# Retention scores in groups that fill four PSUM banks, values of eight heads in one visit, and a new order of work for all engines

## The chip, the cores and the metric

The kernel runs on one NeuronCore of one Trainium2 chip. The metric is the time of one execution on the device in microseconds. All arithmetic is float32.

## The reference, cut to what matters

The input x has 32 sequences of 256 tokens with 128 channels. A first block (L0) normalises x, computes an attention over 128 channels, multiplies it by a gate and adds it to x. A second block (L1) does the same with a retention of 16 heads (width 8 for queries and keys, 16 for values) and with a soft mixture of 8 experts as its gate:

```python
scores = einsum('bhtd,bhsd->bhts', q, k) * mask          # mask: decay, causal, 16 heads
denom  = clip(abs(scores).sum(-1, keepdims=True), 1.0, 50000.0)
ret    = einsum('bhts,bhsv->bthv', scores / denom, v)
ret    = ret * rsqrt(mean(ret * ret, -1) + EPS)
s      = ((xn @ W_g + b_g) * ret) @ W_o + b_o
logits = einsum('bnd,esd->bnes', xn, slots)               # 8 experts x 64 slots
dispatch, combine = softmax(logits, over n), softmax(logits, over all slots)
h   = gelu(einsum('besh', dispatched slots, w1) + b1);  eo = h @ w2 + b2
out = x + s * silu(einsum('bmd,bnm->bnd', eo, combine))
```

Only the retention's scores and values are computed in another grouping after the change; the rest keeps its instructions and gets another place in the order.

## The kernel before

The kernel works on pairs of sequences (512 tokens), 16 pairs in all. Every piece of work on a pair is a small function that issues a few instructions on one engine: `xnT`, `s`, `e`, `score`, `PT`, `local`, `r`, `k`, `v` are the L0 matmuls, `qk`, `gT`, `vg`, `quad`, `g`, `ms`, `o` those of the retention, `LT`, `mxT`, `rB`, `DT`, `slots`, `h`, `eo`, `out` those of the experts. The table `ORDER` (line 53) lists for each of TensorE (PE), VectorE (DVE), ScalarE (ACT) and GpSimd (POOL) the pieces in the order in which that engine issues them, each with an age: in step n of the loop the piece is done for pair n minus age. The loop (`steps_of`) has 18 steps, so a pair is spread over up to three steps and each engine always has three pairs in hand. Every engine is a queue in this written order; a piece waits on semaphores for its inputs (`ready[...]`, `filled[...]`), and whatever stands behind it on its engine waits too. Four PSUM banks of 512 columns (`banks`) are shared out by the table `BANK`; `claim` makes a matmul wait until the last reader of the bank's earlier content is done. The other four banks are one tensor, `bank_s`, for the retention's scores.

The retention of a pair has 32 units (2 sequences x 16 heads), four of them to a quad, 8 quads. Keys are masked by GpSimd into `km`, one 128 x 256 tile a quad (`km_`, line 315), four buffers. `quad` (line 995) makes the scores of four heads: the four heads sit in four groups of 32 rows of the array and write into four banks; for keys 0 to 127 the moving side has 256 queries, for keys 128 to 255 the later 128, so 384 columns of each bank are filled. `ret_` (line 656) multiplies the 4 x 384 columns by the causal mask into `ret`, `ab` (line 476) takes the absolute value into `ret_abs`, `add` (line 323) adds the two key blocks' absolute values on GpSimd. `g` (line 1007) then makes the values (two phases, from `ret`) and the row sums (one phase, from `ret_abs`) of the quad in four groups of 32 columns; two quads share a bank, and `usq`, `den`, `ug`, `rx` read that bank. `ret` and `ret_abs` have two buffers (`MR`), `bank_s` has one: the next `quad` waits for `ret`.

Pieces the text speaks of later: `xn2` (DVE) normalises for L1, `rstd2` and `rnorm` (POOL) its factors, `LTm`, `drec` (DVE), `DTe`, `Dc` (ACT) and `dn` (POOL) make the dispatch softmax before `DT` turns it, `hb` (DVE) adds the bias before `hg` (ACT, Gelu) and `eo` (PE), `eoc` (DVE) takes expert outputs out, `ce` is an Exp, `ln` and `rs` are Ln and Exp of the retention's norm, `tr`, `tv`, `sp`, `zt` are Tanh, `field`, `rvg`, `mix` are DVE instructions with two tensor inputs.

Of the kernel before, what the change touches and what calls it, by code (L numbers as in the profile page):

```python
# [1128 lines left out]
```

## Time and profile before

| | |
|---|---|
| median of 3 runs | 1090.27 us (1090.27 to 1090.41) |
| the profiled execution | 1089.83 us, span 1088.0 us |
| busy of the span | PE 1048.5, weight loads 828.0, DVE 919.0, ACT 806.6, POOL 387.3 us |
| granted TensorE clock | 0.995 over the span |

The span runs from the first to the last instruction. Busy time of PE is modelled from pipelined matmuls, so a high share says that PE always had something in hand, not that it streams at its peak. A float32 matmul of the program is two instructions (passes) in the trace. The profile's page and the answers of the trace give engine, line of the kernel, tiles and shapes for each group.

### The profile page before, as it was taken

Reading aid. Unit: us, or ns where it says so; the run is one execution under the profiler, and the core shown is the slowest. Engines: PE = TensorE matmul, PEld = TensorE weight load, DVE = VectorE, ACT = ScalarE, POOL = GpSimd, SP = SyncE. Lnnn points to the kernel's source line nnn. Section 1 sums busy time; section 2 is a strip of 40 time slices with the busy share of each in tenths; the row PEclk is TensorE's granted clock in tenths of the full one; section 3 lists DMA queues with packets and bytes.
Section 4 is the critical chain, followed back from the end, with each engine's and each line's share of the span. In section 5 each row is a group of like instructions: output and inputs, shape, how many; then the busy total and the mean of one; then the engine's idle time right before and its main releaser. Section 6 shows DMA issues by size and latency. Waiting matters only on the chain.

```text
span 1088.0 us, 27272 instructions
## 1 busy us (share of the span) xinstructions
PE 1048.5 (96%) x10244; PEld 828.0 (76%) x10244; DVE 919.0 (84%) x1818; ACT 806.6 (74%) x1434; POOL 387.3 (36%) x555
## 2 busy tenths in 40 slices
PE   5799999999999999999999999999999999999997
PEld 3478787787878778787786877778787787877866
DVE  3788888988889888997988889888998888989785
ACT  4487877778777786877778777887777868777775
POOL 2432533334343332433335233343433324333240
PEclk9899999999999999999999999999999999999999
DMA  6000000000000000000000000000000000000000
GB/s 257 11 11 2 11 11 2 21 2 11 11 2 21 2 11 11 3 20 2 21 1 12 11 2 20 2 11 11 2 21 2 15 7 11 12 1 12 2 11 11
DMA packets 18463, 16.85 MB, mean 15 GB/s; under 512 B 800, under 2 KB 17440, under 8 KB 18080
## 3 DMA queue, kind: packets, MB, share of 16 engines
q1 hardware_dynamic: 18336, 15.12, 4.3%
q8 instruction: 84, 1.38, 0.5%
q14 instruction: 43, 0.35, 0.1%
HBM read 10.93 MB, written 4.19 MB: 14 GB/s over the span
## 4 chain that ended last, share of the span: by engine, by line
PE 90%; DVE 5%; issue 4%; POOL 1%; ACT 1%; DVEq 0%; POOLq 0%; ACTq 0%
PE bank L969 11%; PE bank L979 11%; PE bank L1023 10%; PE bank_s L1000 7%; PE bank L989 6%; PE bank L960 5%; PE bank L930 5%; PE bank L952 3%; PE bank L910 3%; PE bank L1038 3%; PE bank L825 3%; PE bank L1030 3%; PE bank L876 3%; PE bank L923 3%; PE bank L856 2%
## 5 line engine op out<-in xcount | busy, mean ns | idle before, releaser
L326 POOL TENSOR_TENSOR ret_abs<-ret_abs 128x512 f32<-128x512 f32 x128 | 168.3, 1315 | 435.9 <-ACT ret_abs L479 435.9
L659 DVE TENSOR_TENSOR ret<-bank_s,k_sb 128x1536 f32<-128x1536 f32 x128 | 224.1, 1751 | 5.0 <-PE bank L1023 2.2
L479 ACT ACTIVATE ret_abs<-ret 128x1536 f32<-128x1536 f32 x128 | 189.1, 1477 | 0.5 <-DVE ret L659 0.5
L474 ACT ACTIVATE hact<-hact 128x512 f32<-128x512 f32 x128 | 80.1, 626 | 86.5 <-DVE hact L728 86.1
L979 PE MATMUL bank<-w_sb,hact 128*128 128x128 f32 x1024 | 132.0, 277 | 0.0
L969 PE MATMUL bank<-slotsT,w_sb 128*128 128x128 f32 x1024 | 130.7, 278 | 0.9 <-ACT slotsT L469 0.9
L979 PEld LDWEIGHTS bank<-w_sb,hact 128*128 128x128 f32 x1024 | 124.1, 192 | 8.9 <-ACT hact L474 4.3
L969 PEld LDWEIGHTS bank<-slotsT,w_sb 128*128 128x128 f32 x1024 | 120.6, 192 | 10.2 <-issue 6.6
L1023 PE MATMUL bank<-ret,vrow 128*32 128x256 f32 (+1 forms) x2048 | 108.3, 329 | 0.0
L728 DVE TENSOR_TENSOR hact<-bank,v_sb 128x512 f32<-128x512 f32 x128 | 87.6, 685 | 11.7 <-PE bank L979 8.2
L333 POOL TENSOR_SCALAR dT<-dT,drec 128x256 f32<-128x256 f32 x128 | 64.5, 517 | 91.7 <-DVE drec L723 91.7
L1000 PE MATMUL bank_s<-qT,km 32*128 32x256 f32 x1024 | 91.4, 426 | 0.4 <-issue 0.3
L1023 PEld LDWEIGHTS bank<-ret,vrow 128*32 128x32 f32 x2048 | 59.9, 109 | 41.6 <-issue 2.5
L320 POOL TENSOR_SCALAR km<-kT,k_sb 128x256 f32<-128x256 f32 x128 | 60.0, 483 | 76.7 <-DVE kT L645 76.7
L1023 PE MATMUL bank<-ret_abs,k_sb 128*32 128x256 f32 x1024 | 78.7, 379 | 0.0
L440 ACT ACTIVATE cT<-bank 128x512 f32<-128x512 f32 x64 | 38.2, 598 | 50.5 <-PE bank L930 50.4
L1000 PEld LDWEIGHTS bank_s<-qT,km 32*128 32x128 f32 x1024 | 40.1, 183 | 36.5 <-issue 30.9
L989 PE MATMUL bank<-eorow,cT 128*128 128x129 f32 x512 | 63.9, 278 | 1.0 <-issue 1.0
L455 ACT ACTIVATE dT<-cT,ltmax 128x256 f32<-128x256 f32 x128 | 64.5, 517 | 0.0
L989 PEld LDWEIGHTS bank<-eorow,cT 128*128 128x128 f32 x512 | 59.5, 191 | 3.0 <-issue 1.2
L960 PE MATMUL bank<-d,xn 128*128 128x512 f32 x128 | 57.7, 593 | 0.3 <-ACT d L462 0.3
L462 ACT ACTIVATE d<-bank 128x512 f32<-128x512 f32 x64 | 38.1, 595 | 23.9 <-PE bank L952 23.9
(143 smaller groups left out, 2307.1 us busy)
## 6 DMA issues: line engine op xcount, KB each, us to landing
x_sb<-x SPq DMA_DIRECT2D x16, 256.0 KB, 2.8
w_sb<-w SPq DMA_DIRECT2D x2, 2048.0 KB, 14.2
out<-attn SPq DMA_DIRECT2D x16, 256.0 KB, 2.3
v_sb<-vectors SPq DMA_DIRECT2D x1, 705.0 KB, 7.5
k_sb<-consts SPq DMA_DIRECT2D x1, 538.0 KB, 6.3
w_sb<-weights SPq DMA_DIRECT2D x1, 512.0 KB, 5.0
w_sb<-weights SPq DMA_DIRECT2D x1, 320.0 KB, 3.3
slot_sb<-slot_rows SPq DMA_DIRECT2D x1, 256.0 KB, 3.5
```

What stands on the lines that cost most here:

```text
L326: pool.tensor_tensor(both[:, :, P:SEQ], both[:, :, P:SEQ], both[:, :, SEQ:3 * P], ALU.add)\
L333: ins = pool.tensor_scalar(dT[:, m % 2, b], dT[:, m % 2, b], drec[:, m, b:b + 1], 1.0, ALU.mult, ALU.mult)
L474: act.activation(hact[:, e % 2], hact[:, e % 2], ACT.Gelu).then_inc(ready["hg"].sem, 1)
L479: act.activation(ret_abs[:, q % MR], ret[:, q % MR], ACT.Abs).then_inc(ready["ab"].sem, 1)
L659: dve.tensor_tensor(ret[:, q % MR], bank_s[:, :, 0:3 * P], causal.unsqueeze(1).broadcast_to([P, Q, 3 * P]), ALU.mult)\
L728: dve.tensor_tensor(hact[:, e % 2], bank[:].rearrange("p (c n) -> p c n", c=HC), V["b1"][:, e * HC:(e + 1) * HC].unsqueeze(2).broadcast_to ...
L960: ins = pe.matmul(bank[:], xn3[:, j], d[:, j], start=(i == 0), stop=(i == 1))
L969: ins = pe.matmul(bank[:, c * P:(c + 1) * P], w1_sb[:, e, c * P:(c + 1) * P], slotsT[:, e // 2, 2 * (e % 2):2 * (e % 2) + 2].rearrange("p ...
L979: ins = pe.matmul(bank[:, i * C:(i + 1) * C], hact[:, i, c], w2_sb[:, e, c], start=(c == 0), stop=(c == HC - 1))
L989: ins = pe.matmul(bank[:, i * (C + 1):(i + 1) * (C + 1)], cT[:, m, j * P:(j + 1) * P], eorow[:, m, b], start=(m == 0), stop=(m == E // 2 - 1))
L1000: pe.matmul(bank_s[:, n, 0:SEQ], km[rows, q % KM, 0:P], qT[par][rows, b], start=True, stop=True)
L1023: ins = pe.matmul(bank[n * HT:(n + 1) * HT, into[0]:into[1]], left, src[:, q % MR, n, cols[0]:cols[1]], start=(i == 0 and phase == 0), sto ...
```

## The change

The quads are replaced by six score groups a pair (`scores`, named A in the order). For each sequence the first group holds the 128-key-by-128-query blocks of keys 128 to 255 of all four quads (16 matmuls of 128 columns), the second and third hold the blocks of keys 0 to 127 of two quads each (8 matmuls of 256 columns). Each group fills 4 x 512 columns. `ret`, `ret_abs` become `low`, `low_abs` (4 quads) and `high`, `high_abs` (2 quads), one buffer each. `add` now adds two quads at once (1024 elements a partition), four times a pair. `values` (named gg) issues what two `g` issued, without a break, after one wait.

`ORDER` and `BANK` are written anew for all four engines. `h` 4 to 7, `eo` 2 to 5, the last score group and the last values move from age 2 to age 1, `xn2` and `rstd2` from age 1 to age 0.

```diff
+GROUPS, HALVES = 6, 4
...
-    "PE": [("quad", 7, 2), ("h", 4, 2), ("eo", 2, 2), ("eo", 3, 2), ("h", 5, 2), ("h", 6, 2), ("eo", 4, 2),
...
+    "PE": [("ms", 3, 2), ("xn2T", 0, 1), ("eo", 6, 2), ("qk", 0, 1), ("eo", 7, 2), ("qk", 1, 1), ("xn3T", 0, 1),
+           ("out", 0, 2), ("out", 1, 2), ("LT", 0, 1), ("xnT", 0, 0), ("A", 0, 1), ("LT", 1, 1), ("LT", 2, 1),
+           ("LT", 3, 1), ("A", 1, 1), ("o", 0, 2), ("gT", 0, 1), ("vg", 0, 1), ("vg", 1, 1), ("DT", 0, 1),
+           ("gT", 1, 1), ("DT", 1, 1), ("o", 1, 2), ("s", 0, 0), ("A", 2, 1), ("gg", 0, 1), ("DT", 2, 1),
+           ("DT", 3, 1), ("k", 0, 0), ("global", 0, 0), ("slots", 0, 1), ("ms", 0, 1), ("slots", 1, 1),
+           ("mxT", 0, 1), ("A", 3, 1), ("h", 0, 1), ("gg", 1, 1), ("e", 0, 0), ("h", 1, 1), ("r", 0, 0),
+           ("A", 4, 1), ("rB", 0, 1), ("h", 2, 1), ("ms", 1, 1), ("eo", 0, 1), ("eo", 1, 1), ("h", 3, 1),
+           ("score", 0, 0), ("srow", 0, 0), ("score", 1, 0), ("A", 5, 1), ("gg", 2, 1), ("PT", 0, 0),
+           ("PT", 1, 0), ("v", 0, 0), ("h", 4, 1), ("eo", 2, 1), ("eo", 3, 1), ("local", 0, 0), ("h", 5, 1),
+           ("h", 6, 1), ("ms", 2, 1), ("gg", 3, 1), ("eo", 4, 1), ("eo", 5, 1), ("h", 7, 1)],
+    "DVE": [("hb", 7, 2), ("rx", 3, 2), ("stat", 0, 0), ("xn3", 0, 1), ("eoc", 3, 2), ("qkc", 0, 1), ("qkc", 1, 1),
...
+            ("cs", 0, 1), ("eoc", 0, 1), ("hb", 3, 1), ("smax", 0, 0), ("cs", 1, 1), ("smax", 1, 0),
+            ("srowc", 0, 0), ("ka", 0, 0), ("cs", 2, 1), ("cs", 3, 1), ("ret", 5, 1), ("x2", 0, 2), ("srec", 0, 0),
+            ("rv", 0, 0), ("den", 2, 1), ("hb", 4, 1), ("eoc", 1, 1), ("ug", 2, 1), ("rvg", 0, 0), ("field", 0, 0),
+            ("hb", 5, 1), ("prod", 0, 0), ("x1", 0, 0), ("stat2", 0, 0), ("rx", 2, 1), ("den", 3, 1), ("ug", 3, 1),
+            ("hb", 6, 1), ("xn2", 0, 0), ("eoc", 2, 1)],
+    "ACT": [("dsq", 3, 2), ("hg", 6, 2), ("xn2Tc", 0, 1), ("hg", 7, 2), ("ln", 0, 2), ("xn3Tc", 0, 1),
+            ("rs", 0, 2), ("LTc", 0, 1), ("DTe", 0, 1), ("LTc", 1, 1), ("xnTc", 0, 0), ("LTc", 2, 1), ("ab", 0, 1),
+            ("LTc", 3, 1), ("DTe", 1, 1), ("gTb", 0, 1), ("ab", 1, 1), ("gTb", 1, 1), ("DTe", 2, 1), ("Dc", 0, 1),
+            ("sT", 0, 0), ("DTe", 3, 1), ("Dc", 1, 1), ("zt", 0, 2), ("usq", 0, 1), ("Dc", 2, 1), ("Dc", 3, 1),
+            ("ab", 2, 1), ("slc", 0, 1), ("slc", 1, 1), ("dsq", 0, 1), ("kr", 0, 0), ("hg", 0, 1), ("sgT", 0, 0),
+            ("usq", 1, 1), ("eTc", 0, 0), ("ab", 3, 1), ("hg", 1, 1), ("tr", 0, 0), ("dsq", 1, 1), ("rBc", 0, 1),
+            ("ab", 4, 1), ("hg", 2, 1), ("hg", 3, 1), ("P", 0, 0), ("P", 1, 0), ("ce", 0, 1), ("usq", 2, 1),
+            ("PTc", 0, 0), ("PTc", 1, 0), ("ab", 5, 1), ("tv", 0, 0), ("dsq", 2, 1), ("hg", 4, 1), ("sp", 0, 0),
+            ("hg", 5, 1), ("ce", 1, 1), ("usq", 3, 1), ("ce", 2, 1), ("ce", 3, 1)],
+    "POOL": [("rnorm", 0, 1), ("rstd", 0, 0), ("km", 0, 1), ("km", 1, 1), ("km", 2, 1), ("km", 3, 1),
+             ("mixa", 0, 0), ("dn", 0, 1), ("dn", 1, 1), ("add", 0, 1), ("dn", 2, 1), ("dn", 3, 1), ("km", 4, 1),
+             ("km", 5, 1), ("km", 6, 1), ("km", 7, 1), ("add", 1, 1), ("add", 2, 1), ("add", 3, 1), ("rstd2", 0, 0)],
...
             def add(p, par, h):
+                b, half = divmod(h, 2)
+                pool.wait_ge(*ready["ab"](p, 3 * b))
+                pool.wait_ge(*ready["ab"](p, 3 * b + 1 + half))
+                pool.tensor_tensor(high_abs[:, :, :, P:SEQ], high_abs[:, :, :, P:SEQ], low_abs[:, :, 2 * half:2 * half + 2], ALU.add)\
...
-            def quad(p, par, q):
+            def scores(p, par, a):
+                b, i = divmod(a, 3)
+                quads = range(Q * b, Q * b + Q) if i == 0 else range(Q * b + 2 * i - 2, Q * b + 2 * i)
                 pe.wait_ge(*ready["qkc"](p, 0))
+                pe.wait_ge(*ready["km"](p, quads[-1]))
+                since(pe, ready["ret"], *((p, a - 1) if a else (p - 1, GROUPS - 1)))
+                for u, q in enumerate(quads):
+                    for n in range(Q):
+                        rows = slice(n * HT, (n + 1) * HT)
+                        if i == 0:
+                            ins = pe.matmul(bank_s[:, n, u * P:(u + 1) * P], km[rows, q % KM, P:SEQ], qT[par][rows, b, P:SEQ],
+                                            start=True, stop=True)
+                        else:
+                            ins = pe.matmul(bank_s[:, n, u * SEQ:(u + 1) * SEQ], km[rows, q % KM, 0:P], qT[par][rows, b],
+                                            start=True, stop=True)
+                ins.then_inc(filled["A"].sem, 1)
```

## Rows read from the trace of the kernel before

**Rows 1.** The page, busy time, and the chain that ended last by engine.
```profile
PE 1048.5 (96%) x10244; PEld 828.0 (76%) x10244; DVE 919.0 (84%) x1818; ACT 806.6 (74%) x1434; POOL 387.3 (36%) x555
...
PE 90%; DVE 5%; issue 4%; POOL 1%; ACT 1%; DVEq 0%; POOLq 0%; ACTq 0%
```

**Rows 2.** The waits: who waited for whom, us in total, times, longest.
```profile
PE bank L952 <- POOL dT L333: 12.5, 14, 0.9
```

**Rows 3.** Timeline of PE, 66 us from the middle: start, length, what, times.
```profile
560.60 1.03 PE L916 MATMUL bank<-w_sb,xn2T 128*128 128x256 f32 x4
...
567.40 0.59 PE L930 MATMUL bank<-xn3T,snT 128*128 128x256 f32 x2
567.83 0.59 PE L930 MATMUL bank<-xn3T,slot_sb 128*128 128x256 f32 x2
568.36 0.71 PE L1000 MATMUL bank_s<-qT,km 32*128 32x256 f32 x8
568.89 0.40 PE L1003 MATMUL bank_s<-qT,km 32*128 32x128 f32 x8
569.22 0.70 PE L930 MATMUL bank<-xn3T,snT 128*128 128x256 f32 x2
569.76 0.59 PE L930 MATMUL bank<-xn3T,slot_sb 128*128 128x256 f32 x2
...
575.03 0.86 PE L1023 MATMUL bank<-ret,vrow 128*32 128x256 f32 x16
...
576.79 0.61 PE L1023 MATMUL bank<-ret_abs,k_sb 128*32 128x256 f32 x8
578.29 0.66 PE L952 MATMUL bank<-k_sb,dT 128*128 128x128 f32 x4 [0.89 <-POOL dT L333]
...
609.77 0.69 PE L1030 MATMUL bank<-usq,k_sb 128*128 128x256 f32 x2
610.39 0.71 PE L1000 MATMUL bank_s<-qT,km 32*128 32x256 f32 x8
...
626.40 1.03 PE L916 MATMUL bank<-w_sb,xn2T 128*128 128x256 f32 x4
```

**Rows 4.** Groups by line and shape: busy us, mean ns of one, idle before.
```profile
L659 DVE TENSOR_TENSOR ret<-bank_s,k_sb 128x1536 f32<-128x1536 f32 x128 | 224.1, 1751 | 5.0 <-PE bank L1023 2.2 <-PE bank_s L1003 1.4
L479 ACT ACTIVATE ret_abs<-ret 128x1536 f32<-128x1536 f32 x128 | 189.1, 1477 | 0.5 <-DVE ret L659 0.5
L326 POOL TENSOR_TENSOR ret_abs<-ret_abs 128x512 f32<-128x512 f32 x128 | 168.3, 1315 | 435.9 <-ACT ret_abs L479 435.9
...
L728 DVE TENSOR_TENSOR hact<-bank,v_sb 128x512 f32<-128x512 f32 x128 | 87.6, 685 | 11.7 <-PE bank L979 8.2 <-PE bank L969 2.4
...
L449 ACT ACTIVATE cT<-cT 128x512 f32<-128x512 f32 x64 | 39.8, 622 | 0.2
...
L588 DVE SCALAR_TENSOR_TENSOR spin<-bank,srec,srow 128x128 f32<-128x128 f32 x64 | 18.0, 344 | 8.5 <-PE bank L876 8.5
...
L406 ACT ACTIVATE spin<-spin,v_sb 128x512 f32<-128x512 f32 x16 | 11.3, 708 | 1.6 <-DVE spin L588 1.6
```

**Rows 5.** Timeline of ACT around its table loads.
```profile
550.53 0.61 ACT L474 ACTIVATE hact<-hact 128x512 f32<-128x512 f32 x1
551.16 1.28 ACT L449 ACT_TABLE_LOAD   x1
552.46 0.63 ACT L449 ACTIVATE cT<-cT 128x512 f32<-128x512 f32 x1
...
555.95 0.37 ACT L489 ACTIVATE usq<-bank 128x256 f32<-128x256 f32 x1
556.81 0.42 ACT L493 ACTIVATE den<-den 128x256 f32<-128x256 f32 x1 [0.49 <-DVE den L666]
```

**Rows 6.** Timeline of DVE and POOL: instructions that overlap an `add`, and one that doesn't.
```profile
550.03 2.07 DVE L628 TENSOR_SCALAR xn<-x,mv,rstd 128x128 f32<-128x128 f32 x4
...
550.70 1.31 POOL L326 TENSOR_TENSOR ret_abs<-ret_abs 128x512 f32<-128x512 f32 x1 [1.70 <-ACT ret_abs L479]
...
11.21 1.41 DVE L557 SCALAR_TENSOR_TENSOR mix<-xnT,v_sb,mix 128x512 f32<-128x512 f32 x2 [3.54 <-POOL mix L294]
...
574.02 2.15 DVE L557 SCALAR_TENSOR_TENSOR mix<-xnT,v_sb,mix 128x512 f32<-128x512 f32 x2
```

**Rows 7.** Timeline of PE in the last step, from its last `eo`.
```profile
1074.94 1.16 PE L979 MATMUL bank<-w_sb,hact 128*128 128x128 f32 x8
...
1082.23 1.16 PE L1038 MATMUL bank<-w_sb,ug 128*128 128x128 f32 x8 [0.43 <-DVE ug L687]
```

More of the change, by code:

```diff
@@ L169, in build @@
         qT, kT = ([sb(f"{n}_{i}", 2, SEQ) for i in range(2)] for n in ("qT", "kT"))
-        KM, MR = 4, 2
+        KM = 4
         km = sb("km", KM, SEQ)
         vrow, grow = sb("vrow", TILES, HEADS, HT), sb("grow", 2, TOK)
-        ret, ret_abs = sb("ret", MR, Q, 3 * P), sb("ret_abs", MR, Q, 3 * P)
+        low, low_abs = sb("low", Q, Q, P), sb("low_abs", Q, Q, P)
+        high, high_abs = sb("high", Q, 2, SEQ), sb("high_abs", Q, 2, SEQ)
         usq, den = sb("usq", 2, SEQ), sb("den", 2, SEQ)
@@ L211, in build @@
             ("prod", 1), ("x1", 1), ("stat2", 1), ("mv2", 1), ("var_eps2", 1), ("rstd2", 1), ("rn", 3), ("rnorm", 1),
-            ("xn2", 1), ("xn3", 1), ("xn2Tc", 1), ("xn3Tc", 1), ("qkc", 2), ("km", QUADS), ("vgc", 2), ("gTb", 2), ("ret", QUADS),
-            ("ab", QUADS), ("add", QUADS), ("usq", DUOS), ("den", DUOS), ("dsq", DUOS), ("ug", DUOS),
+            ("xn2", 1), ("xn3", 1), ("xn2Tc", 1), ("xn3Tc", 1), ("qkc", 2), ("km", QUADS), ("vgc", 2), ("gTb", 2), ("ret", GROUPS),
+            ("ab", GROUPS), ("add", HALVES), ("usq", DUOS), ("den", DUOS), ("dsq", DUOS), ("ug", DUOS),
             ("rx", DUOS), ("ln", 1), ("rs", 1), ("gated", 2), ("attn", 2), ("LTc", 4), ("mx", 3), ("rmax", 1), ("rBc", 1), ("cs", 4), ("ce", 4),
@@ L474, in hg, with ab @@
                 act.activation(hact[:, e % 2], hact[:, e % 2], ACT.Gelu).then_inc(ready["hg"].sem, 1)
[L476 to L479 removed]
+            def ab(p, par, a):
+                b, i = divmod(a, 3)
+                act.wait_ge(*ready["ret"](p, a))
+                if i == 0:
+                    since(act, ready["add"], *((p, 1) if b else (p - 1, 3)))
+                    ins = act.activation(low_abs[:], low[:], ACT.Abs)
+                else:
+                    h = 2 * b + i - 1
+                    since(act, filled["gg"], *((p, h - 1) if h else (p - 1, HALVES - 1)))
+                    ins = act.activation(high_abs[:], high[:], ACT.Abs)
+                ins.then_inc(ready["ab"].sem, 1)
             def gTb(p, par, u):
@@ L991, in out_ @@
                 ins.then_inc(filled["out"].sem, 1)
-            def quad(p, par, q):
-                b = q // Q
+            def scores(p, par, a):
+                b, i = divmod(a, 3)
+                quads = range(Q * b, Q * b + Q) if i == 0 else range(Q * b + 2 * i - 2, Q * b + 2 * i)
                 pe.wait_ge(*ready["qkc"](p, 0))
-                pe.wait_ge(*ready["km"](p, q))
-                since(pe, ready["ret"], *((p, q - 1) if q else (p - 1, QUADS - 1)))
-                for n in range(Q):
-                    rows = slice(n * HT, (n + 1) * HT)
-                    pe.matmul(bank_s[:, n, 0:SEQ], km[rows, q % KM, 0:P], qT[par][rows, b], start=True, stop=True)
-                for n in range(Q):
-                    rows = slice(n * HT, (n + 1) * HT)
-                    ins = pe.matmul(bank_s[:, n, SEQ:3 * P], km[rows, q % KM, P:SEQ], qT[par][rows, b, P:SEQ],
-                                    start=True, stop=True)
-                ins.then_inc(filled["quad"].sem, 1)
@@ L1010, in g, with values @@
+                ins.then_inc(filled["A"].sem, 1)
+            def values(p, par, h):
+                b, half = divmod(h, 2)
+                pe.wait_ge(*ready["add"](p, h))
                 pe.wait_ge(*ready["vgc"](p, b))
-                bank = banks[BANK["g", q - 1]] if i else claim("g", p, q)
+                bank = claim("gg", p, h)
                 spread = vrow[:].rearrange("p j h v -> p j (h v)")
-                for phase in range(3):
-                    for n in range(Q):
-                        src = (ret, ret_abs)[phase // 2]
-                        sblock = phase % 2
-                        at = (Q * (q % Q) + n) * HT - i * VD
-                        left = spread[:, 2 * b + sblock, at:at + HT] if phase < 2 else K["count"][:, (1 - i) * VD:(1 - i) * VD + HT]
-                        cols = (0, SEQ) if sblock == 0 else (SEQ, 3 * P)
-                        into = (phase // 2 * SEQ + sblock * P, (phase // 2 + 1) * SEQ)
-                        ins = pe.matmul(bank[n * HT:(n + 1) * HT, into[0]:into[1]], left, src[:, q % MR, n, cols[0]:cols[1]],
-                                        start=(i == 0 and phase == 0), stop=(i == 1 and phase == 2))
@@ L1025, in g @@
-                ins.then_inc(filled["g"].sem, 1)
+                for i in range(2):
+                    for phase in range(3):
+                        for n in range(Q):
+                            at = (Q * (2 * half + i) + n) * HT - i * VD
+                            left = spread[:, 2 * b + phase, at:at + HT] if phase < 2 else K["count"][:, (1 - i) * VD:(1 - i) * VD + HT]
+                            right = (high[:, n, i], low[:, n, 2 * half + i], high_abs[:, n, i])[phase]
+                            into = ((0, SEQ), (P, SEQ), (SEQ, 2 * SEQ))[phase]
+                            ins = pe.matmul(bank[n * HT:(n + 1) * HT, into[0]:into[1]], left, right,
+                                            start=(i == 0 and phase == 0), stop=(i == 1 and phase == 2))
@@ L1027, in ms @@
+                ins.then_inc(filled["gg"].sem, 1)
             def ms(p, par, h):
@@ L1029, in ms @@
                 pe.wait_ge(*ready["ug"](p, h))
-                pe.matmul(banks[BANK["g", 2 * h]][:, SEQ:], K["heads"], usq[:, h % 2], start=True, stop=True)\
+                pe.matmul(banks[BANK["gg", h]][:, SEQ:], K["heads"], usq[:, h % 2], start=True, stop=True)\
                   .then_inc(filled["ms"].sem, 1)
@@ L1056, in _ @@
                           "local": local, "r": r, "k": k_, "v": v, "xn2T": xn2T_, "xn3T": xn3T_, "qk": qk, "vg": vg, "LT": LT,
-                          "mxT": mxT, "rB": rB_, "DT": DT, "slots": slots, "h": h, "eo": eo, "out": out_, "quad": quad, "g": g,
+                          "mxT": mxT, "rB": rB_, "DT": DT, "slots": slots, "h": h, "eo": eo, "out": out_, "A": scores, "gg": values,
                           "gT": gT, "ms": ms, "o": o}, ORDER["PE"],
```

79 lines of the change are left out of this document (35 added, 44 removed), and 33 rows, old and new, of tables (BANK, ORDER).

## The prediction

> **What bounds the kernel now.** I read the page's busy line and the chain first [rows 1]: TensorE is busy for 1048.5 of 1088 us, and 90% of the chain that ended last runs over it. VectorE (84%) and ScalarE (74%) are not the bound, but every piece hands its result through them. Then the waits [rows 2]: in the steady part TensorE waits for one thing, the turning of dT (`DT` 0), 14 times, 12.5 us in all. Then the timeline of a whole step [rows 3]. The same instruction (`vg` 0) starts at 560.60 and 626.40, so a step takes 65.80 us. Of these 0.96 pass between the expected start of `DT` 0 and its actual one: `g` 1 ends its issue at 576.79 + 0.54, `DT` starts at 578.29 (the row says 0.89 idle). About 0.3 more are gaps that busy time hides, such as 0.62 from `ms` 2 (609.77) to `quad` 7 (610.39), where other matmuls of that shape take 0.43 and an entry into a quad 0.10. So TensorE's own stream is 64.54 us a step, 98% of it.
>
> **TensorE's stream after the change.** The rows show what a visit to the small tiles costs [rows 3]. Two full-array matmuls of 256 columns start 0.43 apart (567.40, 567.83). From the last of them to the quad it is 0.53: 0.10 to enter. The quad takes from 568.36 to 569.22, 0.86, where its four passes of four concurrent matmuls stream 2 x 0.216 + 2 x 0.108 = 0.65 (0.216 is half of 0.43); 0.21 are its first, exposed weight load and the drain at its end (256-column part 0.53 instead of 0.43, 128-column part 0.33 instead of 0.22). The next full matmul takes 0.54 instead of 0.43: 0.10 to come back (I take 0.056, half of it, where a transpose follows, whose own start needs less; the bounds are 0 and 0.10).
> - A low group has 8 passes of 128 columns: 8 x 0.109 + 0.215 = 1.09. A high group has 4 of 256: 4 x 0.216 + 0.215 = 1.08. Six groups: 2 x 1.09 + 4 x 1.08 = 6.49, against 8 x 0.865 = 6.92: -0.43. This holds if weight loads within a group stay hidden, as from the 256- to the 128-column part now. The bound from above is a quad's own parts repeated: 0.33 for each quad of a low group, 0.53 for each of a high one, 2 x 1.32 + 4 x 1.17 = 7.3: +0.4. I take the first, since within one visit only the first pass of a quad shows an exposed load.
> - Visits: before, 9 a step (five lone quads, three quads with a `g` pair, one lone pair), 6 of them left into matmuls and 3 into transposes: 9 x 0.093 + 6 x 0.10 + 3 x 0.056 = 1.61. After, from the order, 8: A0, A1, A3, A4, A2+gg0, A5+gg2, gg1, gg3, left 5 times into matmuls and 3 into transposes: 1.42. That is -0.19.
> - The values: `g` pairs stood side by side already and ran without a break (575.03 to 577.33, 2.30), so one visit for eight heads gives nothing on TensorE.
> The stream becomes 64.54 - 0.43 - 0.19 = 63.92 us a step, for 16 pairs 9.9 us less.
> The Trainium skill says in TensorEngine Tiling (Array Packing), Key Properties, that changing the tiling mode drains the array; the rows agree, with 0.10 to enter and 0.10 to leave.
>
> **The other engines.** `ret_` costs 1751 ns for 1536 columns, and 685 for 512 (`hb`, also from PSUM) [rows 4]: 1.04 ns a column, 2.29 us for 2048. 8 x 1.75 - 6 x 2.29 = 0.3 us less on VectorE, beside TensorE. `ab`: 1477 for 1536 and 622 for 512, 0.83 ns a column, 1.90 for 2048: 0.4 less on ScalarE. `add` is four instead of eight, each 2.0 to 2.6 us (from proportional to the second half alone, to twice 1315 ns); I take 2.4. ScalarE's order mixes functions more. Now it loads tables five times a step, each 1.28 us, 1.29 from start to start, and the overlap of neighbours is lost too, 1.4 in all [rows 5]. In the new order changes away from Gelu's table and back stand at hg6, ln, rs, hg0, P, hg4, ce1: seven loads. Four more (`tr`, `hg` 2, `sp`, `hg` 5) come if Tanh doesn't run on Gelu's table, which the trace can't show, since there no Tanh follows a Gelu directly. I take seven, the end nearer to today's five: +2.8 us, with the other end +8.4. ScalarE goes from about 50.4 to 52.8 of 65 us.
> The Trainium skill (ScalarE: Activation LUTs, What ACT_TABLE_LOAD costs) gives 2.66 us for each switch with its drain. By it two more loads would be 5.3 us of ScalarE; the rows show 1.29, and I go by them.
>
> **The new waits.** I laid the new order out with these lengths, counting from the start of `ms` 3: A0 ends at 10.9, A1 starts at 13.7 and ends at 14.7, A2 starts at 21.9, gg0 at 23.0, A3 31.6 to 32.7, gg1 33.8, A4 38.9 to 40.0, A5 46.8 to 47.9, gg2 47.8, `local` ends at 56.4, gg3 58.8, `eo` 6 is due at 64.7.
> - Score to score: A1 needs `ret` 0, 10.9 + 0.2 + 2.3 = 13.4. Slack 0.3, the smallest; the others have over 3.
> - Score to values: hand-over 0.2, `ret` 2.3, `ab` 1.9, `add` 2.4, 6.8 in all. gg0 has 8.3 for it, gg1 10.8, gg2 7.8, gg3 10.9. What stands before `ab` 1 (`gTb` 0) and `add` 0 (`dn` 1) fits. They hold.
> - `DT`: `dn` 0 comes 4 us before `DT` 0, `dn` 1 1 us before `DT` 1. The wait of 0.96 goes. `slots` 0 behind `Dc` 3 has 0.1 of slack, the banks of A2's neighbour `s` (behind `gTb` 1) 0.3.
> - The seam of the step. From the end of `local` (56.4) ScalarE and VectorE must do, one after the other: `field` 4 x 0.28 (18.0 us for 64), 1.1, `sp` 0.7, `hg` 5 0.6, a load 1.3, `ce` 1 0.55, `usq` 3 0.3, `ce` 2 and 3 1.1, `dsq` 3 0.3, a load 1.4, `hg` 6 0.6 [rows 4, 5]: 8.0. `eo` 6 is due 8.3 later. But `field` stands behind `rvg`, which has two SBUF inputs, and that behind `add` 3. By my layout `ret` 5 ends at 52.4 (`cs` 2, `cs` 3, `ka` before it), `ab` 5 at 54.3, `add` 3 at 56.8, so `rvg` ends at 57.5 and `field` at 58.5, 1.0 late. `eo` 6 starts about 0.8 late, and behind it are `qk`, `out` and everything. `xn2`, also behind this, is 0.4 late for `xn2T`, inside the same delay.
> - The port. An instruction of VectorE with two SBUF inputs, or a fast one, stretches while an `add` runs: `mix` takes 2.15 beside one and 1.41 alone, and the four of `xn2` 2.07 [rows 6]. After the change an `add` blocks up to 2.4 us at once, four times. Outside the seam I find it beside `mx` and `cs` 1, each with cover, and price the rest at 0.2 on the path (0 to 1).
> The Trainium skill (SBUF — State Buffer, Terms, shared port pair) says the port is held exclusively for a whole instruction. The 0.74 us that `mix` loses agree, and the rule speaks against wider adds: half as many, each worst case twice as long.
> New waits are thus 0.8 + 0.2 + 0.1 for the thin seams, 1.1, against 1.26 before. A step becomes 63.92 + 1.1 = 65.0.
>
> **Ends.** The first 33 us are L0 alone in both. The new order puts `k` before `e`. In this start `mix` ends at 12.6 [rows 6], so `k` waits for nothing long but puts itself ahead of `e`, up to 2 us; ScalarE's one-time squares of the slots stand behind `eTc` and cover part of it. I take +0.5 between 0 and 2. The tail from the last `eo` (1074.94) to the end is the same chain of `eoc`, `out`, `z`, `zt`, `x2` (13.1 us [rows 7]); `o` has the same place in it.
>
> **Sum.** Stream -9.9, waits 15 steps x -0.16 = -2.4, ends +0.5, thin seams in step 16, where L0's work no longer covers, +0.5: -11.3. The profiled execution of 1089.83 becomes 1078.5; the median is 0.44 above the profiled time, so 1079.
>
> **Rivals.**
> 1. The seam closes (adds at 2.0, `field` on time) and only 0.2 of waits is left: step 64.1, -1.7 x 15, 1089.8 - 25.5 + 1 + 0.4 = 1066. For it: my chain is 8.0 of 8.3 without the port. Against: it leaves nothing for a late `ret` 5, and VectorE has three pieces ahead of that. Chance 0.15.
> 2. Slower: Tanh between two Gelus costs its own loads. `hg` 4, `sp`, `hg` 5 then carry two more loads, 2.8 us, in the chain that already ends last at the seam, so nearly all of it is on the path: step 65.0 + 2.6 = 67.6, +1.8 x 15 = +27, 1117. It decides as soon as `sp` has its own load; half of it would do. For it: ScalarE's order has 11 changes of function. Against: it needs a switch that no row of this trace has. 0.12. A smaller version: `add` and two-input instructions meet at three or four seams for 0.8 each instead of one; step 66.6, 1103. 0.09.
> 3. A new wait of the old one's size takes its place (a second thin seam opens by 0.7): 65.7 a step, about 1090. 0.07.
> 4. The wide groups don't hide their loads: +0.4 instead of -0.43, 0.8 a step more, 1092. 0.07.
> My forecast, 1079 with its own range 1071 to 1086, has 0.50.
>
> **Numbers.** No change is within 0.2% (2.2 us). Faster: forecast and rival 1 and a little of 3, 0.69. Same: 0.08. Slower: 0.23. The range 1064 to 1100 takes in rivals 1, 3 and 4 and leaves out the loads of Tanh and extremes, 0.2.
>
> **What would show it.** Right: score groups of 1.09 and 1.08 from start to next start, 8 visits; steps of about 65.0 us; no wait at `DT` 0; a wait of 0.8 at `eo` 6 for hact from ScalarE; seven loads a step (112 in all). Wrong: eleven loads, groups of 1.3, `add` over 2.6 us, or TensorE waiting for `ret_abs` at `gg`.

## The result, and the profile after

The changed kernel takes 1103.3 us (median of 4 runs, 1102.95 to 1105.08) beside 1090.27 for the kernel before (1089.97 to 1090.41): ratio 1.0124, 95% interval 1.0109 to 1.0139. It is slower, where 1079 was forecast, and outside the range. The profiled execution took 1103.20, span 1101.4.

The page of the kernel after, busy time and the chain [rows 1]; then TensorE's waits [rows 2]:
```profile
PE 1049.2 (95%) x10244; PEld 812.3 (74%) x10244; DVE 903.5 (82%) x1786; ACT 851.5 (77%) x1434; POOL 383.6 (35%) x491
...
PE 4%; DVE 1%; ACT 1%; issue 0%; POOL 0%; POOLq 0%; DVEq 0%; ACTq 0%
```
```profile
PE bank L844 <- DVE xn L639: 15.5, 16, 7.0
...
PE bank L1044 <- DVE spin L599: 4.3, 15, 0.3
PE bank L998 <- DVE eorow L758: 3.1, 15, 0.2
```
The chain breaks off after 6% of the span, so this time it tells nothing. In the waits the one of 12.5 us at `DT` is gone, and three have come at the seam of the step: `xn2T` (L844) for `xn2` on VectorE (15.5 less the 7.0 of the first pair, so 15 of 0.57), `gg` 3 (L1044) for `field` (L599), `eo` 6 (L998) for VectorE's `eoc`.

The timeline of PE after: a high group, a low group (each with the instruction behind it, for the pitch) and the seam [rows 3]:
```profile
584.18 1.15 PE L1025 MATMUL bank_s<-qT,km 32*128 32x256 f32 x16
585.25 0.64 PE L1044 MATMUL bank<-high,vrow 128*32 128x256 f32 x8
...
620.88 0.60 PE L1051 MATMUL bank<-usq,k_sb 128*128 128x256 f32 x2
621.75 0.64 PE L1044 MATMUL bank<-high,vrow 128*32 128x256 f32 x8 [0.28 <-DVE spin L599]
...
626.83 0.60 PE L1051 MATMUL bank<-usq,k_sb 128*128 128x256 f32 x2
627.98 0.66 PE L844 MATMUL bank<-k_sb,xn 128*128 128x128 f32 x4 [0.55 <-DVE xn L639]
628.85 1.13 PE L998 MATMUL bank<-w_sb,hact 128*128 128x128 f32 x8 [0.21 <-DVE eorow L758]
...
1054.87 1.17 PE L1022 MATMUL bank_s<-qT,km 32*128 32x128 f32 x32
1055.97 1.16 PE L988 MATMUL bank<-slotsT,w_sb 128*128 128x128 f32 x8
```
A high group takes 1.07, a low one 1.10. `ms` 3 starts at 560.76 in one step and 626.83 in the next: 66.07. That step, and the mean of steps 2 to 15 (65.97; steps are counted from 0 to 17), stand against 65.80. To split such a step into stream and waits I gave each piece its usual pitch (start to next start where nothing is waited for) and summed what was above it; before that gives 64.54 + 1.26, after 63.93 + 2.03.

| us of the span | before | after | change | forecast |
|---|---|---|---|---|
| stream of all steps | 1032.6 | 1022.9 | -9.7 | -9.9 |
| waits, steps 2 to 15 | 17.6 | 28.5 | +10.9 | -2.4 |
| first `xn2T` starts at | 32.85 | 36.76 | +3.9 | +0.5 with the next row |
| waits, step 1 | 4.80 | 5.92 | +1.1 | |
| waits, steps 16 and 17, with 1.6 of a lower clock (see the two buffers) | 9.97 | 17.15 | +7.2 | +0.5 |
| sum | | | +13.4 | -11.3 |

Groups of the kernel after by line and shape (busy, mean ns of one, idle before) [rows 4, 5]:
```profile
L330 POOL TENSOR_TENSOR high_abs<-high_abs,low_abs 128x1024 f32<-128x1024 f32 x64 | 158.2, 2472 | 369.4 <-ACT high_abs L489 369.4
L678 DVE TENSOR_TENSOR high<-bank_s,k_sb 128x2048 f32<-128x2048 f32 x64 | 146.5, 2289 | 27.3 <-PE bank L1044 17.6 <-PE bank_s L1025 9.6
L489 ACT ACTIVATE high_abs<-high 128x2048 f32<-128x2048 f32 x64 | 122.2, 1909 | 27.1 <-DVE high L678 25.0
...
L478 ACT ACT_TABLE_LOAD x48 | 61.6, 1283 | 0.9
...
L618 DVE SCALAR_TENSOR_TENSOR prob<-prob 128x512 f32<-128x512 f32 x16 | 25.8, 1613 | 0.7 <-ACT prob L426 0.7
```
The wide instructions have the lengths of the forecast (`add` 2.47, `ret` 2.29, `ab` 1.91), and the tables are loaded seven times a step. The last row is the loss: `rvg` takes 1.61 us in the mean, where its kind takes 0.68. The timelines of DVE and POOL at the seam show why [rows 6]:
```profile
618.91 1.66 DVE L618 SCALAR_TENSOR_TENSOR prob<-prob 128x512 f32<-128x512 f32 x1
620.49 1.11 DVE L599 SCALAR_TENSOR_TENSOR spin<-bank,srec,srow 128x128 f32<-128x128 f32 x4
```
```profile
617.66 2.36 POOL L330 TENSOR_TENSOR high_abs<-high_abs,low_abs 128x1024 f32<-128x1024 f32 x1 [8.11 <-ACT high_abs L489]
```
`add` 3 runs to 620.02. `rvg` starts at 618.91 and ends 0.55 after it. `field`, the next in VectorE's queue, starts at 620.49. `local`, which it reads, starts at 617.30 on TensorE, and in the first run below `field` starts 1.99 after `local` does; so here it is some 1.2 late, and `prod`, `x1`, `stat2`, `rstd2` and `xn2` follow it one by one.

### The profile page after: what moved, and what is told of

It is laid out like the page before. It is cut to its first block and busy times, and to the rows that moved or that the text cites. A ratio compares the mean times of both kernels' runs of the same rounds, so it can differ in the third digit from the quotient of the medians.

```text
span 1101.4 us, 27081 instructions
## 1 busy us (share of the span) xinstructions
PE 1049.2 (95%) x10244; PEld 812.3 (74%) x10244; DVE 903.5 (82%) x1786; ACT 851.5 (77%) x1434; POOL 383.6 (35%) x491
## 5 line engine op out<-in xcount | busy, mean ns | idle before, releaser
L330 POOL TENSOR_TENSOR high_abs<-high_abs,low_abs 128x1024 f32<-128x1024 f32 x64 | 158.2, 2472 | 369.4 <-ACT high_abs L489 369.4
L678 DVE TENSOR_TENSOR high<-bank_s,k_sb 128x2048 f32<-128x2048 f32 x64 | 146.5, 2289 | 27.3 <-PE bank L1044 17.6
L489 ACT ACTIVATE high_abs<-high 128x2048 f32<-128x2048 f32 x64 | 122.2, 1909 | 27.1 <-DVE high L678 25.0
L998 PEld LDWEIGHTS bank<-w_sb,hact 128*128 128x128 f32 x1024 | 122.6, 192 | 22.0 <-issue 13.8
L998 PE MATMUL bank<-w_sb,hact 128*128 128x128 f32 x1024 | 130.0, 278 | 3.6 <-DVE eorow L758 3.1
L673 DVE TENSOR_TENSOR low<-bank_s,k_sb 128x2048 f32<-128x2048 f32 x32 | 73.3, 2291 | 21.6 <-PE bank L1044 17.8
L1044 PE MATMUL bank<-high,vrow 128*32 128x256 f32 x1024 | 80.7, 385 | 5.4 <-DVE spin L599 4.3
L1044 PE MATMUL bank<-high_abs,k_sb 128*32 128x256 f32 x1024 | 79.5, 379 | 0.0
L1025 PE MATMUL bank_s<-qT,km 32*128 32x256 f32 x1024 | 73.3, 400 | 1.5 <-DVE low L673 1.5
L485 ACT ACTIVATE low_abs<-low 128x2048 f32<-128x2048 f32 x32 | 61.4, 1917 | 13.6 <-DVE low L673 13.6
L844 PE MATMUL bank<-k_sb,xn 128*128 128x128 f32 x256 | 40.7, 283 | 23.5 <-DVE xn L639 15.5
L844 PEld LDWEIGHTS bank<-k_sb,xn 128*128 128x128 f32 x256 | 31.5, 144 | 42.2 <-DVE xn L639 21.7
```

The costliest lines, as they stand in the source:

```text
L330: pool.tensor_tensor(high_abs[:, :, :, P:SEQ], high_abs[:, :, :, P:SEQ], low_abs[:, :, 2 * half:2 * half + 2], ALU.add)\
L489: ins = act.activation(high_abs[:], high[:], ACT.Abs)
L673: ins = dve.tensor_tensor(low[:].rearrange("p n i m -> p (n i) m"), flat.rearrange("p (u m) -> p u m", m=P), causal[:, 2 * P:3 * P].unsque ...
L678: ins = dve.tensor_tensor(high[:].rearrange("p n i m -> p (n i) m"), flat.rearrange("p (u m) -> p u m", m=SEQ), causal[:, 0:SEQ].unsqueeze ...
L844: ins = pe.transpose(bank[:, j * P:(j + 1) * P], src[:, j], ident)
L998: ins = pe.matmul(bank[:, i * C:(i + 1) * C], hact[:, i, c], w2_sb[:, e, c], start=(c == 0), stop=(c == HC - 1))
```

## The experiments

Step lengths are means of steps 2 to 15 of the profiled execution, times the medians; each ratio is to the kernel before on the same chip.

**One swap on VectorE.**
```diff
-            ("rv", 0, 0), ("den", 2, 1), ("hb", 4, 1), ("eoc", 1, 1), ("ug", 2, 1), ("rvg", 0, 0), ("field", 0, 0),
+            ("rv", 0, 0), ("den", 2, 1), ("hb", 4, 1), ("eoc", 1, 1), ("ug", 2, 1), ("field", 0, 0), ("rvg", 0, 0),
```


> The kernel after with one edit: on VectorE field goes ahead of rvg. Theory A (the port: rvg stands beside add 3 and stretches from 0.69 to 1.66 us, and field, which reads PSUM, waits behind it): in every step the 0.36 us before the last values visit goes, the waits at ms 3, xn2T and eo 6 (1.3 us together) shrink by 0.6 to 0.9, the step falls from 65.98 to about 64.9 and the time from 1103 to about 1087. Theory B (ScalarE's table loads at the seam are the bound): the step changes by less than 0.3 us, 1099 to 1103.

Measured: 1090.78 us (1089.04 to 1092.67), ratio 1.0012 [1.0003, 1.0022]; the step 65.01. The timeline of DVE in it:
```profile
611.75 1.13 DVE L599 SCALAR_TENSOR_TENSOR spin<-bank,srec,srow 128x128 f32<-128x128 f32 x4 [0.29 <-PE bank L895]
612.79 0.68 DVE L618 SCALAR_TENSOR_TENSOR prob<-prob 128x512 f32<-128x512 f32 x1
```
`field` reads PSUM and starts as soon as `local` is done; `rvg` comes after the `add` and takes 0.68. The wait at `gg` 3 (0.35 a step) is gone, and that at `xn2T` is 0.13 instead of 0.73 (`ms` 3 starts at 618.94 and `xn2T` at 619.50, where 0.43 is the usual pitch). So the order of two names in one list gives back 12.5 us; the step is now 0.79 shorter than before, and the longer ends use that up.

**A short add at the seam.** The fourth `add` of a pair works on an eighth of its elements; the rest of that sum is left out.
```diff
+                w = P // 8 if h == 3 else P
+                pool.tensor_tensor(high_abs[:, :, :, P:P + w], high_abs[:, :, :, P:P + w], low_abs[:, :, 2 * half:2 * half + 2, 0:w], ALU.add)\
```


> The kernel after, with the add of the last values of a pair (add 3) leaving out seven eighths of its elements, so that it holds the port for some 0.5 us instead of 2.36; the order is the one of the kernel after. Theory A (the port): rvg takes 0.69 again, the step falls by about 1.0 to 65.0, the time to about 1088. Theory B (table loads or GpSimd's own chain of rstd2): no change beyond 0.3 us a step.

Measured: 1091.84 us (1089.13 to 1092.14), ratio 1.0014 [1.0005, 1.0023], with `rvg` still ahead of `field`; the step 65.07, and 64.97 without step 7, which the part on two instructions that start together (below) explains. The row of `rvg`:
```profile
614.45 0.68 DVE L619 SCALAR_TENSOR_TENSOR prob<-prob 128x512 f32<-128x512 f32 x1
```
Moved out of the way or the `add` made short, the gain is the same: it is the meeting of the two that costs, not the order as such.

**Two buffers of `high` and `high_abs`.** To have room, one expert's w1 serves all eight; the others' are left out.
```diff
-        high, high_abs = sb("high", Q, 2, SEQ), sb("high_abs", Q, 2, SEQ)
+        high, high_abs = sb("high", 2, Q, 2, SEQ), sb("high_abs", 2, Q, 2, SEQ)
-                    since(dve, filled["gg"], *((p, h - 1) if h else (p - 1, HALVES - 1)))
+                    since(dve, filled["gg"], *((p, h - 2) if h >= 2 else (p - 1, HALVES - 2 + h)))
```


> The kernel after with two buffers each for high and high_abs, so that ret of a high group no longer waits for the values before it. To make room all experts use the first w1 (the others are left out). Theory A (single buffers cost mainly in step 16, where L0's work is gone): the steady step stays at 65.9 to 66.0, step 16 falls from 63.8 to about 61.5, the time by 2 to 3 us. Theory B (single buffers set the steady step): the step falls by 0.5 or more, the time by 8 or more.

Measured: 1114.39 us (1112.3 to 1114.56), ratio 1.0222 [1.0207, 1.0237]: slower by 11 us than the changed kernel. Step 16 fell from 63.78 to 61.26, but the steady step rose to 66.80. No theory had that. DVE, POOL and PE around it:
```profile
598.79 3.44 DVE L726 TENSOR_TENSOR mx<-mx,cT 128x512 f32<-128x512 f32 x2
```
```profile
599.32 2.38 POOL L330 TENSOR_TENSOR high_abs<-high_abs,low_abs 128x1024 f32<-128x1024 f32 x1 [1.47 <-ACT high_abs L489]
```
```profile
602.29 0.65 PE L957 MATMUL bank<-k_sb,mx 128*128 128x128 f32 x4 [0.61 <-DVE mx L726]
```
With its buffer free the second `add` starts 0.26 ahead of the second `mx`, and this takes 2.66 us instead of 0.69 (their two lengths by tile are 685 and 2655 ns); `mxT` waits for it.

Of the 2.5 us that step 16 fell, only 0.9 belong to the buffers. `h` 5 waits 1.10 instead of 2.00 there, while A4 still waits 1.49 and `gg` 2 1.18. The other 1.6 are TensorE's clock: in the profiled execution of the changed kernel the granted clock is 0.74 from 1075 to 1080 us and 0.92 from 1080 to 1085, so part of that stretch ran at 1.2 GHz and not at 2.4. The run with the old start (below) has the same order in this step, waits the same 2.00 at `h` 5, and keeps a clock of 1.00; its step 16 takes 62.17. Here are `h` 5 and 6 in the changed kernel, and in that run:
```profile
1077.24 3.59 PE L988 MATMUL bank<-slotsT,w_sb 128*128 128x128 f32 x16 [2.00 <-DVE eorow L758]
```
```profile
1077.09 2.02 PE L996 MATMUL bank<-slotsT,w_sb 128*128 128x128 f32 x16 [2.00 <-DVE eorow L770]
```

**The same with that add short** (its second `add` of a pair on an eighth, the rest of the sum left out too).
```diff
+                w = P // 8 if h == 1 else P
```


> The kernel with two buffers of high (one expert's w1 for all, the others' left out), and in it the second add of each pair on an eighth of its elements, the rest of that sum left out. In the trace of the two-buffer kernel the second instruction of mx took 2.66 instead of 0.69 us while that add ran (599.32 to 601.70), and the matmul mxT waited for it. Theory A (the port: the buffer's wait held add 1 off mx before, and without it the two meet): the wait of 0.78 at mxT goes, the steady step falls from 66.80 to 66.0, the kernel from 1114.4 to 1101 to 1104. Theory B (the earlier abs and ret of the two-buffer kernel push something else on ScalarE or VectorE ahead of mxT): mx takes 0.69 again but the step stays at 66.6 or more, 1112 to 1114.

Measured: 1102.71 us (1102.56 to 1102.97), ratio 1.0123 [1.0106, 1.014]; the step 65.97. The same two instructions:
```profile
593.07 1.56 DVE L727 TENSOR_TENSOR mx<-mx,cT 128x512 f32<-128x512 f32 x2
```
The second `mx` takes 0.77 here, and both together took 3.44 before. So the 11.7 us between the two runs were the meeting at the port. A wait that holds a GpSimd `add` back can be worth more than the buffer that takes the wait away.

**Two instructions that start together.** The changed kernel has this meeting too. In its steady steps the second `mx` starts 0.06 to 0.08 ahead of `add` 1 (592.09 and 592.15), keeps its 0.69, and the `add` is the one that takes longer, 2.84 instead of 2.36, for which TensorE doesn't wait. In step 7 the two start within 0.01 of each other. The `mx` came first there in the profiled executions of the changed kernel, the swap and the one with old order and banks, and the `add` in those of the short add, the old start and the five loads. A usual step of the kernel with five loads, then its step 7, on VectorE and GpSimd:
```profile
390.68 1.48 DVE L726 TENSOR_TENSOR mx<-mx,cT 128x512 f32<-128x512 f32 x2
455.75 3.67 DVE L726 TENSOR_TENSOR mx<-mx,cT 128x512 f32<-128x512 f32 x2
```
```profile
391.54 2.84 POOL L330 TENSOR_TENSOR high_abs<-high_abs,low_abs 128x1024 f32<-128x1024 f32 x1 [2.11 <-ACT high_abs L489]
456.54 2.34 POOL L330 TENSOR_TENSOR high_abs<-high_abs,low_abs 128x1024 f32<-128x1024 f32 x1 [2.11 <-ACT high_abs L489]
```
The second `mx` takes 2.88 there, `mxT` waits 1.21, and the step takes 66.43 instead of 65.0. So this order has a meeting whose winner is set by less than 0.1 us, and 1.4 us hang on it wherever it is lost. The three pieces moved below part the two by 0.7 us, and with them no step of this kind is left.

**The start in the old order.** Step 0 runs the L0 pieces in the order of the kernel before (`e` ahead of `k`, `PT` 0 ahead of `srow`), and `claim` waits for whoever really held the bank.
```diff
+START = {"PE": [("xnT", 0, 0), ("s", 0, 0), ("e", 0, 0), ("global", 0, 0), ("r", 0, 0), ("k", 0, 0), ("score", 0, 0),
...
-                for name, k, age in order:
+                for name, k, age in (ORDER if step else START)[engine]:
```


> The kernel after, but the first step, in which there is only L0 of the first pair, is issued in the order of the kernel before (e ahead of k, PT ahead of srow); each bank claim waits for the bank's actual last holder. Theory A (the new order of L0 costs 3.9 us once at the start): xn2T of the first pair starts at about 33.0 instead of 36.8, the time falls by 3.5 to 4, the steps stay at 65.98. Theory B (the start is hidden behind the loads of the experts' weights): no change beyond 0.5 us.

Measured: 1101.35 us (1100.98 to 1101.87), ratio 1.0107 [1.0092, 1.0122]. The first `xn2T` starts at 35.20: 1.56 of the 3.9 are the order. The step is 66.07, and 65.95 without step 7, in which the `mx` lost (67.38); step 16 is 62.17 at a full clock.

**And in the old banks.** Under the new `BANK` `PT` and `srow` share a bank, `v` and `local` another. Here the first pair's L0 pieces have those of before.
```diff
+BANK0 = {('PT', 0): 0, ('PT', 1): 2, ('e', 0): 3, ('global', 0): 0, ('k', 0): 0, ('local', 0): 1, ('r', 0): 1, ('s', 0): 1, ('score', 0): 1, ('score', 1): 2, ('srow', 0): 1, ('v', 0): 0, ('xnT', 0): 3}
```


> The kernel after with the first step in the order of the kernel before and also with that kernel's banks for L0 of the first pair (with the order alone, PT and srow shared a bank and so did v and local). Theory A (order and banks of L0 are the whole 3.9 us of the start): xn2T of the first pair starts at 32.9 and the span falls by 3.9 from 1101.4. Theory B (something else): it stays at 35.2, as with the order alone.

Measured once: 1097.54 us beside 1089.46 for before (no interval). The first `xn2T`, in the changed kernel, with the old order, and with order and banks:
```profile
36.76 1.11 PE L844 MATMUL bank<-k_sb,xn 128*128 128x128 f32 x4 [7.02 <-DVE xn L639]
```
```profile
35.20 1.12 PE L852 MATMUL bank<-k_sb,xn 128*128 128x128 f32 x4 [7.02 <-DVE xn L651]
```
```profile
33.14 1.12 PE L858 MATMUL bank<-k_sb,xn 128*128 128x128 f32 x4 [7.01 <-DVE xn L657]
```
The start is explained to 0.3 us: the order 1.6, the shared banks 2.1.

**Five table loads instead of seven.** On top of the swap, `ce` 1 and 2 stand behind `PTc` 1 and `ce` 3 behind `tv`, so no Exp parts two Gelus.
```diff
-            ("hg", 5, 1), ("ce", 1, 1), ("usq", 3, 1), ("ce", 2, 1), ("ce", 3, 1)],
...
+           ("PTc", 1, 0), ("ce", 1, 1), ("ce", 2, 1), ("ab", 5, 1), ("tv", 0, 0), ("ce", 3, 1), ("dsq", 2, 1),
```


> field ahead of rvg as before, and ScalarE's ce 1, 2, 3 moved ahead of hg 4, so that Gelu's table stays from hg 4 to hg 7: five table loads a step instead of seven. Theory A (VectorE's line to xn2 paces the step, ScalarE's loads matter only for eo 6): the wait behind xn2T (0.42 + 0.16) shrinks by up to 0.4, the step falls from 65.01 to 64.6 to 65.0. Theory B (the loads pace it): the step falls to 64.3 or below, the time to 1080.

Measured: 1088.71 us (1088.3 to 1090.5), ratio 0.9998 [0.9989, 1.0008]; ScalarE loads five times a step and the step stays 65.0 (65.11 with step 7, in which the `mx` lost) with the same waits. `eo` 6, which waited for ScalarE's `hact` in the swapped kernel, now waits as long for VectorE:
```profile
620.36 1.13 PE L998 MATMUL bank<-w_sb,hact 128*128 128x128 f32 x8 [0.20 <-ACT hact L478]
```
```profile
623.84 1.13 PE L998 MATMUL bank<-w_sb,hact 128*128 128x128 f32 x8 [0.20 <-DVE eorow L758]
```
Two loads less are 2.6 us of ScalarE a step and nothing on the path of the steady step. Step 16 takes 61.56 instead of 63.15 and step 17 14.72 instead of 15.08. But the whole 1.6 of step 16 arise in matmuls at a lower clock that only the profiled execution of the swapped kernel has (0.92 from 1060 to 1065 us and 0.73 to 1070, where the five-load kernel has 1.00), so 0.4 us in step 17 are what the loads gave back; how much of the 2.1 us between the medians is theirs stays open.

**Three pieces moved.** On top of that: `attn` 1 behind `drec` 2 (it stood ahead of what `DT` 3 waits for), `x2` behind `sg`, `dsq` 0 behind `Dc` 3.
```diff
-            ("vgc", 0, 1), ("vgc", 1, 1), ("attn", 1, 2), ("mx", 0, 1), ("LTm", 3, 1), ("drec", 2, 1),
...
+           ("vgc", 0, 1), ("vgc", 1, 1), ("mx", 0, 1), ("LTm", 3, 1), ("drec", 2, 1), ("attn", 1, 2),
```


> The kernel with few loads, and three pieces moved on VectorE and ScalarE into idle stretches: attn 1 behind mx 0, LTm 3 and drec 2 (it waited 1.9 us for o 1 with DT 3's inputs behind it), x2 out of the stretch ahead of xn2 to right behind sg, dsq 0 ahead of ab 2. Theory A (waits of the new order are seams, each ended by one late piece): the 0.24 at DT 3 and the 0.25 at ms 3 go, the step is 64.0 to 64.3, the time 1075 to 1078. Theory B (VectorE's whole load is the bound): the step stays above 64.8.

Measured: 1082.89 us (1081.96 to 1084.14), ratio 0.9942 [0.9927, 0.9957]. The step is 64.72, between the two theories: the 0.24 at `DT` 3 are gone, the 0.13 at `xn2T` behind `ms` 3 are not, and `eo` 6 still waits 0.42.

**All of it, with the old start** (the edits of the last three headings and of the two on the start together).
```diff
-                return banks[BANK[name, k]]
+                return banks[bank_at(name, k, p)]
```


> The kernel with the moved seams and with the start of the kernel before (order and banks in the first step). The two savings add up: 3.9 us less than that kernel, 1071 to 1074.

Measured: 1079.32 us (1078.64 to 1079.71), ratio 0.9906 [0.989, 0.9923]: the fastest whole version, under the kernel before and the changed one. The old start gave 3.6 here too; the expectation was too low because it counted on a shorter seam. Its page, and the seam on PE and DVE:
```profile
PE 1043.1 (97%) x10244; PEld 807.9 (75%) x10244; DVE 921.5 (85%) x1786; ACT 808.4 (75%) x1402; POOL 381.0 (35%) x491
```
```profile
614.27 0.60 PE L1065 MATMUL bank<-usq,k_sb 128*128 128x256 f32 x2
614.84 0.66 PE L858 MATMUL bank<-k_sb,xn 128*128 128x128 f32 x4
615.69 1.13 PE L1012 MATMUL bank<-w_sb,hact 128*128 128x128 f32 x8 [0.20 <-DVE eorow L776]
```
```profile
607.07 1.13 DVE L617 SCALAR_TENSOR_TENSOR spin<-bank,srec,srow 128x128 f32<-128x128 f32 x4 [0.47 <-PE bank L909]
```
What is left is a chain of hand-overs: VectorE sits idle for 0.47 until `local` is out of TensorE, and from `field` over `sp`, `prod`, `x1`, `stat2` and `rstd2` to `xn2` (613.67) every piece needs the one before. `local` earlier would shorten it, and so might `sp` ahead of `hg` 4, behind which it stands for 0.3 on ScalarE; neither was tried.

**All adds short in that version** (each on an eighth, the rest of the sums left out), to see what the port still holds.
```diff
+                w = P // 8
```


> The best kernel so far (field ahead of rvg, five table loads, three pieces moved, the old start), all four adds of a pair on an eighth of their elements, the rest of the sums left out: what is left of the port and of the length of add in it. Theory A (the adds now lie beside cover everywhere in the steady part; the step's last wait is the chain from local over field, stat2 and rstd2 to xn2): 64.6 to 64.72 a step, 1077 to 1079.5. Theory B (adds still stretch pieces on the path): the step falls to 64.3 or less, 1073 or less. Step 16 may gain up to 1 us in both, since there gg 1 and gg 2 wait for add.

Measured: 1077.81 us (1076.78 to 1078.66), ratio 0.9894 [0.9879, 0.9909]. The step is 64.71, the same; step 16 falls from 60.68 to 59.38. In the steady state four adds of 2.4 us now cost nothing.

**The grouping in the order of before.** The wide groups and eight-head visits laid, by my hand, into the order and banks of the kernel before (A0 to A2 where quads 0 to 2 stood, no work moved between ages; `e`, which stood behind `g` 1 and `DT` 0, was put ahead of `gg` 0).
```diff
...
+           ("qk", 1, 1), ("gT", 0, 1), ("vg", 0, 1), ("xn3T", 0, 1), ("out", 0, 2), ("A", 0, 1), ("out", 1, 2),
+           ("LT", 0, 1), ("LT", 1, 1), ("A", 1, 1), ("LT", 2, 1), ("xnT", 0, 0), ("LT", 3, 1), ("gT", 1, 1),
+           ("vg", 1, 1), ("s", 0, 0), ("A", 2, 1), ("e", 0, 0), ("gg", 0, 1), ("DT", 0, 1), ("global", 0, 0),
...
```


> Grouping alone: the two wide score groups and the eight-head value visits, laid into the order and the PSUM banks of the kernel before (A0 to A2 behind quads 0 to 2, DT0 ahead, field work as before, no early rope). Theory A (the grouping itself is worth its own stream, measured as 1032.6 to 1022.9 us, and the loss of the changed kernel comes from its new order): the stream falls by about 9.7 us, the waits stay near the 55.4 us of before plus what the single score buffers and the longer chain of gg ask for, up to 1 us a step; 1080 to 1095 us, step 65.1 to 66.0, first transpose of xn2 near 32.9, last two steps about 83 together. Theory B (the grouping brings the waits: one buffer of each height leaves exponentials, adds and score groups in a row whatever the order): 1100 us or more, a step of 66.0 or longer, with the waits at the score groups and at gg.

Measured: 1198.87 us (1196.36 to 1199.43), ratio 1.0998 [1.098, 1.1017]; the step 72.17. TensorE's waits in it:
```profile
PE bank L888 <- ACT probT L399: 23.1, 15, 1.5
PE bank L857 <- ACT sT L370: 21.9, 15, 1.5
PE bank_s L1018 <- DVE low L666: 18.8, 17, 1.6
```
Its stream, by the same sum of pitches, is 63.93 a step, that of the changed kernel: the saving belongs to the grouping and not to the order. Its waits are 8.2 a step. The two longest, 3.0 together, are L0's matmuls `local` and `e` behind ScalarE, where an `ab` of 1.9 stands ahead of what they need, and 1.1 are A4 behind `ret` 3. The wait of `e` (1.5) comes at the place that I gave it. The upper bound of the first theory was missed by 104 us. This is one layout among many, so it doesn't show that every order near the old one loses, nor what the new order costs; it shows that the grouping can't simply be dropped into the old order.

## Why the prediction was wrong, step by step

- **The stream: right.** Forecast 64.54 to 63.92; measured 63.93, groups 1.10 and 1.07 against 1.09 and 1.08. Weight loads inside a wide group stay hidden. Rival 4 falls; its price was also too high, since two parts of 0.53 are 1.06 and not 1.17, so that bound gives 6.9 us for the groups, what the quads took, and not 7.3.
- **Lengths and loads: right.** `ret` 2.29, `ab` 1.91, `add` 2.47 against 2.4; seven loads a step, so Tanh follows Gelu without one, and rival 2's large version falls. That the loads cost nothing on the steady path is shown by the run with five.
- **The wait at `DT` 0: right, gone.** `DT` 3 has a new one of 0.24 behind `attn` 1. The layout had looked at `dn` 0 and 1 only.
- **The seam: the step that failed.** It said "`field` at 58.5, 1.0 late. `eo` 6 starts about 0.8 late", and of `xn2` "0.4 late for `xn2T`, inside the same delay". The place and the partners (`rvg` behind `add` 3, `field` behind it) were right, and so was the size at `field`, 1.2 late against 1.0. What the delay then does to TensorE was wrong in three ways. The stretched `rvg` sits in a chain that runs over VectorE to `xn2`, not over ScalarE to `hg` 6, and I had walked only the second with its 8.0 us. `xn2T` waits 0.73, `eo` 6 0.42 and `qk` 0 0.16, one behind the other and not one inside the other. And `gg` 3 waits 0.35 for `field`, since its bank is the one `field` reads; I had not laid the banks out. With 0.24 at `DT` 3 these are 1.9 of the 2.03. The term of the sum that was too small is thus the new waits, forecast at 1.1 a step. The swap shows that 0.96 of it is the meeting with `add` 3. The wait forecast at `eo` 6 for ScalarE's `hact` is one for VectorE's `eoc` instead.
- **The ends: failed.** "+0.5" for the start, with `k` ahead of `e` as the only cause. Shown: 1.6 by the order, 2.1 by banks that L0's pieces share, another thing that I had not laid out for a step without other work. The 1.1 of step 1 stays open. "+0.5" for step 16: 7.2 for steps 16 and 17, of which 1.6 are the lower clock. There A4 waits 1.49 for `ret` 3, which waits for `gg` 1 to free `low`, and `gg` 2 waits for `add` 2; `h` 5 waits 2.00 for a bank that `eoc` 1 frees, behind `ret` 5, which waits for `gg` 2. The single buffers that have cover in the steady state are bare in the last steps:
```profile
1062.00 1.15 PE L1025 MATMUL bank_s<-qT,km 32*128 32x256 f32 x16 [1.49 <-DVE low L673]
...
1070.00 0.64 PE L1044 MATMUL bank<-high,vrow 128*32 128x256 f32 x8 [1.19 <-POOL high_abs L330]
```
  The second buffers take 0.9 of it away, short adds 1.3 (measured in the best version), five loads 0.4; what the rest splits into stays open.
- **Rival 2's smaller version** gave the time, 1103, for "`add` and two-input instructions meet at three or four seams". They meet at one that matters, worth 0.96 a step, and 11.2 of the 24.7 us between the forecast and the profiled time are the ends (12.2 against 1.0, and 1.6 of the 12.2 are the clock). That its 1103 was hit is luck: a smaller loss in the steps and a larger one at the ends add up to it.

The forecast of 1079 is what the best version takes, but not by the forecast's terms: its step is 64.72 and not 65.0, and its steps 16 and 17 are 5.5 us longer than before and not 0.5. The stream's saving is there, and the new order as written gave it away at one meeting on the port, one piece ahead of `DT` 3, the start and the last two steps.

## What to carry to other kernels

Lay out a reordered kernel with its banks and buffers for the first and last steps too, where nothing covers a hand-over. Follow each delay at a seam through every engine that leads to the matmuls behind it, and add waits that stand one after the other. Before widening a GpSimd instruction, or giving it a second buffer, list VectorE's two-input SBUF instructions in its window and put PSUM readers there instead. Where two of them start within a tenth of a microsecond, part them, or the time will hang on which comes first.
